# Batching the small transposes of an SSD chunk loop, and moving two scalings from ScalarE to VectorE, in an eight-core hybrid-layer kernel

## What is computed

```python
zxbcdt = einsum('bld,df->blf', layernorm(x), in_proj_w)
z, xBC, dt = split(zxbcdt, [2048, 2048 + 2304])
xBC = silu(causal_conv4(xBC, conv_w) + conv_b)
x_part, B, C = split(xBC, [2048, 2048 + 128])      # 32 heads of 64; state width 128
dt = softplus(dt + dt_bias);  A = -exp(A_log)
def scan_fn(state, inp):                            # over the 4096 positions
    dt_t, x_t, B_t, C_t = inp
    state = state * exp(A * dt_t) + outer(x_t * dt_t, B_t)
    return state, einsum('bhpn,bn->bhp', state, C_t)
y = scan(...) + x_part * repeat(D, 64)
g = y * silu(z);  g = g * rsqrt(mean(g**2) + eps) * norm_w
x = x + g @ out_proj_w
```

## Time and profile before

| what | us |
|---|---|
| median of the runs | 10936.94 (2 runs, 10922.43 to 10951.44) |
| the profiled execution's own time | 10956.51 |
| its span on core 4, the slowest | 10955.0 |
| spans of all cores | 10854.1 to 10955.0 |
| median span of the dies | 10907.7 and 10940.8 |

### The profile page before, as it was taken

The page is one execution under the profiler, slowest core; times in us unless marked ns, Lnnn a source line. Parts: engine busy times, 40 slices in busy tenths (PEclk is TensorE's granted clock), DMA queues, the critical chain, the costliest instruction groups (busy, mean ns, idle before and its releaser), DMA issues.

```text
span 10955.0 us, 95553 instructions; the slowest of 8 cores (10854.1 to 10955.0 us)
## 1 busy us (share of the span) xinstructions
PE 5487.8 (50%) x20462; PEld 2030.0 (19%) x20656; DVE 3510.9 (32%) x6988; ACT 3165.2 (29%) x6832; POOL 148.6 (1%) x234
## 2 busy tenths in 40 slices
PE   0335445454554545435443666566666666634543
PEld 0112222222222222211111222111111111111211
DVE  0434434343443434335531323322111101024430
ACT  0113241423324142310010111244556575700002
POOL 2000000000000000000000000000000000000000
PEclk9996657575665757567666767566677787756665
DMA  6331101010110101021023222100000000020013
GB/s 96 77 83 32 38 15 53 1 53 21 32 38 15 53 1 53 8 47 47 31 59 81 72 70 72 56 28 28 28 16 12 28 1 28 1 61 32 31 52 110
DMA packets 377980, 454.19 MB, mean 41 GB/s; under 512 B 121633, under 2 KB 214434, under 8 KB 377378
## 3 DMA queue, kind: packets, MB, share of 16 engines
q1 hardware_dynamic: 288914, 393.56, 11.5%
q0 software_dynamic: 88528, 54.52, 3.2%
HBM read 348.17 MB, written 136.64 MB: 44 GB/s over the span
## 4 chain that ended last, share of the span: by engine, by line
PE 32%; DVE 23%; ACT 17%; issue 12%; DMA 11%; DVEq 2%; SPq 1%; ACTq 1%; POOL 1%; POOLq 0%
PE pB L191 9%; ACT pt_sb L191 9%; PE pA L191 7%; PE pE L191 6%; PE pF L191 4%; DVE accf L191 4%; PE pC L191 3%; DVE y L191 3%; PE pD L191 3%; ACT Uall L191 2%; DVE t1b L191 2%; ACT Xtall L191 2%; DVEq L189 2%; DMA wtmp<-win_l 2%; DMA ocm<-xres 1%
## 5 line engine op out<-in xcount | busy, mean ns | idle before, releaser
L191 DVE TENSOR_TENSOR pt_sb<-pt_sb,mask01b 128x128 bf16<-128x128 bf16 x512 | 115.1, 225 | 1866.1 <-ACT pt_sb L191 1865.0
L191 PE MATMUL pB<-pt_sb,vb 128*65 128x512 bf16 (+3 forms) x1152 | 509.4, 442 | 356.8 <-ACT pt_sb L191 291.3
L191 ACT ACTIVATE pt_sb<-pE,ebias 128x512 bf16<-128x512 f32 x576 | 382.0, 663 | 887.6 <-PE pE L191 807.1
L191 PE MATMUL pA<-pt_sb,vb 128*65 128x512 bf16 (+3 forms) x1152 | 518.8, 450 | 108.6 <-DVE pt_sb L191 31.1
L191 ACT ACTIVATE Uall<-pT,dtT 128x64 bf16<-128x64 bf16 x1024 | 319.1, 312 | 622.3 <-PE pT L191 534.8
L191 ACT ACTIVATE sig_t<-pA 128x512 bf16<-128x512 f32 x32 | 19.1, 597 | 1406.4 <-PE pA L191 1406.3
L191 ACT ACTIVATE pt_sb<-pF,ebias 128x512 bf16<-128x512 f32 x576 | 382.0, 663 | 89.9 <-PE pD L191 6.0
L191 PE MATMUL pA<-r_t,wr_sb 128*128 128x512 bf16 x246 | 87.6, 517 | 635.6 <-DVE h L191 635.2
L191 PE MATMUL pE<-qq_sb,K_sb 64*128 64x512 bf16 x576 | 263.9, 458 | 261.2 <-DVE den_t L191 189.4
L191 ACT ACTIVATE pt_sb<-pC,ebias 128x512 bf16<-128x512 f32 (+1 forms) x576 | 368.4, 640 | 85.3 <-PE pC L191 0.4
L191 ACT ACTIVATE pt_sb<-pD,ebias 128x512 bf16<-128x512 f32 (+1 forms) x576 | 368.4, 640 | 84.8
(11 more groups left out here) (303 smaller groups left out, 10243.9 us busy)
## 6 DMA issues: line engine op xcount, KB each, us to landing
winm<-winb_h SPq DMA_DIRECT2D x272, 256.0 KB, 2.6
wq_sb<-wqkvb_h SPq DMA_DIRECT2D x192, 256.0 KB, 2.6
xrtB<-xres SPq DMA_DIRECT2D x16, 2048.0 KB, 8.8
xres<-xrtB SPq DMA_DIRECT2D x16, 2048.0 KB, 7.6
xrtC<-xres SPq DMA_DIRECT2D x16, 2048.0 KB, 11.5
xtm<-x SPq DMA_DIRECT2D x32, 512.0 KB, 4.5
xres<-xcs SPq DMA_DIRECT2D x32, 512.0 KB, 3.5
xrt<-xres SPq DMA_DIRECT2D x8, 2048.0 KB, 12.4
```

The lines of the kernel that those rows point to most:

```text
L191: ins = getattr(h, ent[1])(*ent[2], **ent[3])
```

## The change

It edits three places of the chunk loop and nothing else.

- U/X stage: eight transposes go side by side into the eight 128-column slots of T1, then eight into T2, with one wait for the bank ahead of each eight. The 64 ScalarE scalings become four VectorE multiplications of 128 x 1024, two for each bank, whose second operand is the column of 16 head scales, each repeated 64 times (`colrep`, which `tYb` uses too). The event `w_ux` and the banks' events move to VectorE.
- Decay stage: the eight transposes of a group are all issued before the first ScalarE instruction. Heads 4 to 7 use columns 256:384 of the four banks, so only heads 0 to 3 wait for a bank. ScalarE waits for TensorE once in each group, for the last of the eight, where it waited eight times before; a bank is free after the instruction of its second head.
- y2 stage: eight transposes go into T1 and eight into T2, and VectorE waits for TensorE once for each eight.

```diff
-            for c2 in range(16):
-                bkt = "T1" if c2 % 2 == 0 else "T2"
-                w = bgw(c, bkt) + [w_conv[c2]]
-                if w_uxread is not None and c2 == 0:
-                    w.append(w_uxread)
-                S.op("tensor", "transpose", pb[bkt][:, 0:128],
-                     xav(c2, qsl), c.idb, waits=w)
+            for bi, bkt in enumerate(("T1", "T2")):
+                for sl8 in range(8):
+                    c2 = bi * 8 + sl8
+                    w = bgw(c, bkt) + [w_conv[c2]] if sl8 == 0 else [w_conv[c2]]
+                    if w_uxread is not None and c2 == 0:
+                        w.append(w_uxread)
+                    S.op("tensor", "transpose", pb[bkt][:, sl8 * 128:(sl8 + 1) * 128],
+                         xav(c2, qsl), c.idb, waits=w)
                 w6 = S.ms("tensor")
-                for half in range(2):
-                    h = 2 * c2 + half
-                    S.op("scalar", "activation", Uall[:, h * 64:(h + 1) * 64],
-                         pb[bkt][:, half * 64:(half + 1) * 64], AF.Copy,
-                         scale=dtT[:, hb + h:hb + h + 1],
-                         waits=[w6] if half == 0 else [])
-                    S.op("scalar", "activation", Xtall[:, h * 64:(h + 1) * 64],
-                         pb[bkt][:, half * 64:(half + 1) * 64], AF.Copy,
-                         scale=sc2T[:, hb + h:hb + h + 1])
-                bgs(c, bkt, S.ms("scalar"))
-            w_ux = S.now("scalar")
+                hb2 = bi * 16
+                S.op("vector", "tensor_mul",
+                     v3(Uall[:, hb2 * 64:(hb2 + 16) * 64], 16, 64),
+                     v3(pb[bkt][:, 0:1024], 16, 64),
+                     colrep(dtT, hb + hb2, 16), waits=[w6])
+                S.op("vector", "tensor_mul",
+                     v3(Xtall[:, hb2 * 64:(hb2 + 16) * 64], 16, 64),
+                     v3(pb[bkt][:, 0:1024], 16, 64),
+                     colrep(sc2T, hb + hb2, 16))
+                bgs(c, bkt, S.ms("vector"))
+            w_ux = S.now("vector")
...
-                        w = bgw(c, bk)
-                        S.op("tensor", "transpose", pb[bk][:, 128:256],
+                        slo = 128 + (hh // 4) * 128
+                        w = bgw(c, bk) if hh < 4 else []
+                        S.op("tensor", "transpose", pb[bk][:, slo:slo + 128],
                              fbc(cumcT[:, hb + h:hb + h + 1]), c.idf, waits=w)
-                        w7 = S.ms("tensor")
-                        w2 = [w7] + ([w_e4] if (hh == 0 and w_e4 is not None) else [])
+                    w7 = S.ms("tensor")
+                    for hh in range(8):
+                        h = hg * 8 + hh
+                        bk = "EFCD"[hh % 4]
+                        slo = 128 + (hh // 4) * 128
+                        w2 = ([w7] + ([w_e4] if w_e4 is not None else [])) if hh == 0 else []
                         S.op("scalar", "activation", D4[:, hh * 128:(hh + 1) * 128],
-                             pb[bk][:, 128:256], AF.Relu,
+                             pb[bk][:, slo:slo + 128], AF.Relu,
                              bias=cumcT[:, hb + h:hb + h + 1], scale=-1.0, waits=w2)
-                        bgs(c, bk, S.ms("scalar"))
+                        if hh >= 4:
+                            bgs(c, bk, S.ms("scalar"))
+                        else:
+                            S.ms("scalar")
...
-            for c2 in range(16):
-                bkt = "T1" if c2 % 2 == 0 else "T2"
-                w = bgw(c, bkt)
-                S.op("tensor", "transpose", pb[bkt][:, 128:256],
-                     ypra[:, c2 * 128:(c2 + 1) * 128], c.idb, waits=w)
+            for bi, bkt in enumerate(("T1", "T2")):
+                for sl8 in range(8):
+                    c2 = bi * 8 + sl8
+                    w = bgw(c, bkt) if sl8 == 0 else []
+                    S.op("tensor", "transpose", pb[bkt][:, sl8 * 128:(sl8 + 1) * 128],
+                         ypra[:, c2 * 128:(c2 + 1) * 128], c.idb, waits=w)
                 w11 = S.ms("tensor")
                 w_yprtp_last = w11
-                S.op("vector", "scalar_tensor_tensor",
...
+                for sl8 in range(8):
+                    c2 = bi * 8 + sl8
+                    S.op("vector", "scalar_tensor_tensor",
+                         y2[:, c2 * 512:(c2 + 1) * 512][:, qsl],
+                         xav(c2, qsl),
+                         c.drep_sb[:, c2:c2 + 1], pb[bkt][:, sl8 * 128:(sl8 + 1) * 128],
+                         ALU.mult, ALU.add, waits=[w11] if sl8 == 0 else [])
+                    w_y2[(qq, c2)] = S.ms("vector")
+                bgs(c, bkt, w_y2[(qq, 15 if bi else 7)])
```

## The result

| what | before | after |
|---|---|---|
| median of the runs shown with the result, us | 10925.46 (10 runs, 10870.12 to 10972.78) | 10472.69 (11 runs, 10446.93 to 10547.69) |
| ratio | | 0.9593, 95% interval 0.9565 to 0.962 |
| the profiled execution's own time | 10956.51 | 10447.5 |
| its span, slowest core | 10955.0 (core 4) | 10446.0 (core 3) |

The change makes the kernel 4.1% faster.

A forecast was written before the change was run, and what follows sets the result against it. The prediction took the chunk loop's chain of engine hand-overs as the bound, no engine being full: 10.55 + 1.05 + 1.0 = 12.6 us a chunk, x 32 = 403 us saved, giving 10,540 us, range 10,495 to 10,665.

The forecast's parts named there:

- First D: Start of the decay stage: forecast 11.1 us after the first x transpose, against 21.85 before.
- Stage from first D to last exponential: Decay stage: forecast 19.4 us in place of 20.45, a gain of 1.05 us a chunk.
- D spacing: Decay stage, ScalarE instructions of a group: starts 0.46 us apart with one wait each, against 0.515 before.
- y spacing: y2 stage, VectorE instructions: starts 0.46 us apart with one wait each, against 0.52 before.
- The new wait at the border of two groups: Decay stage: later heads' transposes wait for bank D to be freed, losing 0.16 us at each of three borders.
- second wait: Decay and y2 stages: forecast cost 0.055 to 0.07 us each; rival says free, 10,615 us, chance 0.12.
- PSUM-and-repeat form: U/X multiplications on VectorE: forecast 1.22 us each; rival says double column cost, 2.3 us each, 10,670 us, chance 0.04.
- The f32 transposes: Decay stage: forecast 0.22 us apart; rival says no pipelining, 0.45 us each, 10,650 us, chance 0.05.
- The clock in the dense stretches: z blocks and out-projection: forecast unchanged; rival says TensorE stays at 1.2 GHz, costing 436 us, 10,970 us, chance 0.03.
- the sum of a chunk: Chunk loop: gains of the three edited stages, 10.55 + 1.05 + 1.0 = 12.6 us a chunk.
- part 1: U/X stage edit: forecast to gain 10.55 us a chunk in the mean.
- part 2: Decay stage edit: forecast to gain 1.05 us a chunk, or lose 0.5 if the spacing stayed 0.515.

The follow-up runs named there:

- e7: Changed kernel with one more, long-satisfied TensorE wait ahead of 28 D and 14 y instructions a chunk; median 10587.6 us, chunk 53.58 us.
- e1: Kernel before with only the U/X stage edit; median 10458.1 us, chunk 50.97 us, ratio 0.959 to the kernel before.
- e2: Kernel before with only the decay stage edit; median 10928.4 us, chunk 64.85 us, ratio 1.0015 to the kernel before.
- e5: Changed kernel with the decay stage edit undone; median 10482.9 us, chunk 49.96 us.
- e4: Kernel before, unedited, run again for a second trace; median 10908 us.
- e11: Kernel before, unedited, run a third time; median 10879 us.
- e8: Changed kernel with decay transposes, D and exponentials issued ahead of the chain, in more buffers; median 9983.8 us, ratio 0.9153 to the kernel before.

## Why the prediction was off, step by step

**Right: where the time is.** The chunk loop was taken as one chain, 32 times, with all cover named. First D 11.1 us after the first transpose: 11.05. Stage from first D to last exponential 19.4: 1861.13 to 1880.47, 19.34. Multiplication 1.22: 1.21 to 1.23. D spacing 0.46: 0.46; y spacing 0.46: 0.45. The new wait at the border of two groups, 0.16 us: 0.14, the idle bracket of the first D of a group reading 0.34 for TensorE's pD in place of 0.20 for ScalarE's exponential. A chunk of 51 us: 50.92.

**Right: the rivals turned down.** The second wait is not free (e7). VectorE took no longer for the PSUM-and-repeat form, 1.21 to 1.23, than for Gm with its inputs in SBUF, 1.225. The f32 transposes follow by 0.22. The clock in the dense stretches is 1.00 as before (the earlier trace rows holds four windows, not the five that the prediction counts; all read 0.50).

**Too small: the sum of a chunk**, 12.6 us against 12.88 (13.0 with the fourth chunks), by 9 us (13) over 32 chunks. Among the terms U/X gave 10.8 in the followed chunk (10.7 expected), the decay stage 1.1 (1.05), y2 1.0 (1.0).

**Badly described: the share of the parts.** The sum put 10.55 us on the U/X part and 1.05 on the decay part. Done alone, the U/X part gives 12.8 (e1); the decay part costs 1.0, alone (e2) and within the whole (e5), for its wait for eight transposes lies ahead of the first D, which stands 2.2 us later for it (8.8 in e5, 11.05 in the changed kernel). The prediction worked that wait out (9.64 to 11.1) but booked it under part 1, and so never said that the kernel would be better off without part 2.

**Wrong: the outside of the loop, the base, and the range.** The step that failed is the last one, from the chunk to the kernel's time. Of the 67 us, 11.5 come from the median of before, which was 10936.9 in two runs and 10925.5 in ten; 6 from rounding 10,534 up to 10,540; 13 from the chunk (with the fourth chunks); and 37 from outside the loop (453 - 416), where I had expected nothing and, what was worse, had given the range no width: its bounds held unknown costs of the chunk only. The same program scatters by 100 us from run to run (10870 to 10973), in part by the clock (the execution of 10957 us stood at 0.81 for 519 to 1095 us, e4's of 10878 never), and two medians of the kernel before, e4's 10908 and e11's 10879 on another chip, lie 29 us apart. Some 11 of the 37 were the luck of this pair of sets (453 against 442 in the mean of three); the other 26 (20 by the traces) stay open, as told above.

## What to carry to other kernels

Where the windows of a stage show no engine full, add up the chain of hand-overs instead of busy times, and book each delay under the edit that causes it: part of a change can then be seen to cost time while the whole gains. Many small instructions that pace each other cost a wait each on top of their work, so turning 64 into four can pay even where it makes the engine that takes them the busier one (VectorE 22.66 to 27.20 us a chunk, ScalarE 32.55 to 15.99); the next step is to let the engines that take turns run side by side (e8). A range needs the scatter of the whole kernel in it, not only the unknown terms of the change.

## What the runs showed of the hardware

A second wait in front of an instruction, though long satisfied, cost 0.055 us on ScalarE and 0.07 on VectorE (e7 against the changed kernel: D spacing 0.515 and 0.46, y spacing 0.52 and 0.45). In the packed chunk of e8 the granted clock was 0.65 in the window shown (0.53 to 0.65 over its chunks), and TensorE's busy time for the same 162 matmuls 15.85 us against 21.30 at 0.50; in the chunks of the kernel before it had stayed at 0.50, in those of the changed kernel at 0.50 to 0.53. In four of the thirteen traces (e4's and the three of the changed kernel) the clock never stood at 0.81; in the other nine it did on some or all cores, for up to 1520 us on one. At 0.81 eight matmuls of 512 columns took 2.27 us (before, core 0), at 1.00 they took 1.89 (changed, core 0). The length of a stretch that nothing edits goes with the clock that it happens to be granted: 1046 us at a mean of 0.67, 1089 at 0.63.
